# A sparse expert layer behind attention: the last batch's routing chain moved to earlier steps, pair numbers copied by another engine, the last combines paired

## The chip, the cores and the metric

The kernel runs on one core of a Trainium2 chip. The metric is the device time of one launch in microseconds. The median of three runs of the kernel before is 531.6 us (531.27 to 532.24).

## What is computed

The input x has 4 batches of 512 tokens with 256 features (2048 tokens). Three residual parts follow one another: half of a feed-forward layer, attention, and half of the same feed-forward layer again. Cut to what matters:

```
x = x + 0.5 * ffn(layernorm(x))
x = x + attention(layernorm(x))          # 3 heads, full 256 features each
x = x + 0.5 * ffn(layernorm(x))
ffn(x): scores = sigmoid(x @ gate_w)                     # 16 experts
        selected = top_2(scores + expert_bias)
        w = scores[selected] / sum(scores[selected])
        shared = silu(x @ sg) * (x @ su) @ sd            # every token
        routed = sum over the 2 selected e of w_e * (silu(x @ g_e) * (x @ u_e)) @ d_e
        return shared + routed
```

All products are done in three passes over a high and a low part of each float32 operand, so that they are near to full float32.

## The kernel before, in words

The work is written out by hand as one program for each of the five engines: TensorE (PE), VectorE (DVE), ScalarE (ACT), GpSimd (POOL) and SyncE (SP, which only issues DMAs). Each executes its list in order; semaphores tie them together. The change lies in the second feed-forward layer ("FFN 2"), behind the attention.

**Tiles.** The tokens are sorted by expert into tiles of 128 rows. With 2048 tokens and 2 experts each there are 47 tiles at most. FFN 2 handles them in two phases. Tiles 0 to 8 (`FULL_TILES` = 9) hold only tokens of batches 0 to 2 and can start before batch 3's experts are known. Tiles 9 to 46 hold the rest. In a loop step s (function `ffn` of each engine) PE transposes the rows of tile s, multiplies tile s - 1 by the expert's gate and up weights, transposes the product of tile s - 3 and multiplies tile s - 4 by the down weights. ACT copies the high parts and applies Silu; DVE makes the low parts and the products. ACT copies the result of a tile to `y_buf` (L1039), and POOL scatters it to `pair_dram` by pair number (`scatter_y`, L1935). `between(s)` at the end of a step runs side work.

**Rows.** The normalised rows of each token are written by indirect DMAs of POOL into slabs in DRAM, one slab for each expert (`slab_row`, L1906: 4 tiles of tokens, twice, as each token has two experts). Beside the 256 features a row holds its pair number, which POOL puts there first (`mark`, L1889 and L1890). SP loads one tile of rows at a time (`load_row`, L2114) into a ring of 4 buffers; the load of tile n waits until PE has transposed tile n - 4 and until `keep_id(n - 4)` (POOL, L1929) has copied that tile's pair numbers out of the buffer. Before the tiles of phase 2 are loaded, SP writes 17 blocks of zero rows behind the ends of the slabs (`clear_rest`, L2120 and L2126), once DVE has given their addresses (`zero_at`, L1360).

**Batch 3's routing chain** runs beside phase 1, as side work of the steps (function `late_front` on PE, ACT and DVE). In order: DVE normalises the 4 row tiles (L1224, step 1); PE transposes them (`late_turn`, steps 2 and 3), ACT and DVE split them (`front_hi` L919, `front_lo` L1253); PE multiplies by the router (`front_router`, step 4); ACT applies Sigmoid (`front_sigmoid`, L934, step 4) and at once a one-element Silu, to have Silu's table loaded again (L1063); PE transposes the scores (step 5); DVE picks the two experts (`choose`, steps 5 to 7); PE counts ranks (`rank_again`, step 8); DVE makes slab addresses (`slab_rows`, steps 8 and 9, ends at L1344) and the table of tiles (`tile_table(True)`, steps 10 and 11). PE turns the table over (`pack_table`, behind phase 1), DVE writes it (`write_table`, L1421).

**The shared expert.** The same engines handle the shared expert batch by batch: `shared_gu` (gate and up), ACT's `shared_silu`, DVE's `shared_mul` (L1261), `shared_hi` and `shared_lo` (L965, L1265), PE's `shared_y`, and DVE's `shared_sink` (L1278). PE does `shared_gu(1, 0)` in step 9 and `shared_gu(1, 1)` in step 10 of phase 1, and behind its last step 12 `shared_y(1, 0)`, `shared_gu(1, 2)`, `pack_table(True)`, `shared_y(1, 1)`, `shared_y(1, 2)`, and then phase 2. The inputs of batches 1 and 2 are reloaded from DRAM by SP (`reload_batch`, L2071); ACT copies their high part (`back_hi`, L925), and POOL makes the low part (`back_lo`, L1923), for which `shared_gu` of that batch waits.

**POOL's list in FFN 2** is: `keep_id` 0 to 3; `back_lo(1)`; `keep_id(4)`; `scatter_y(0)`; `keep_id(5)`; `scatter_y(1)`; `back_lo(2)`; `keep_id(6)`; `scatter_y(2)`; `keep_id` 7 and 8; `scatter_y(3)`; the 8 `slab_row`s; `scatter_y` 4 to 8; then one `keep_id` and one `scatter_y` for each tile of phase 2.

**The tail.** When 39 tiles are scattered, SP loads the pairs of the first 12 token tiles (`load_pair`, L2134, 256 KB each), when all 47 are, those of the last 4. DVE combines: two operations for each token tile (L1529), the second waiting for the first. SP stores each token tile to the output when it is combined (`tail2`, L2165).

## Time and profile before

| | us |
|---|---|
| median of 3 runs (531.27 to 532.24) | 531.6 |
| the profiled execution | 529.91 |
| its span, first to last instruction | 528.7 |
| PE busy in the span | 443.9 (84%) |
| DVE busy | 334.8 (63%) |
| POOL busy | 299.0 (57%) |
| ACT busy | 266.1 (50%) |

The mean granted clock of TensorE over the span is 0.956 of full speed. The profile is of one execution, taken by the hardware. Times are microseconds from the first instruction. PE is TensorE's matmuls, PEld its weight loads. SPq is the issue of a DMA on SP's queue. In the rows of a timeline, the first number is the start, the second the length (several alike are merged, their count is behind the x), and square brackets give the idle time ahead and what ended it.

### The profile page before, as it was taken

The page shows a single profiled execution, that of the slowest core. Times are in us where ns is not written, and L with a number is a line of the kernel's source. Part 1 is how long each engine was busy: PE and PEld are TensorE (multiplying, and loading weights), DVE is VectorE, ACT ScalarE, POOL GpSimd, SP SyncE. Part 2 cuts the span into 40 slices and gives each one's busy share as a digit, 9 for nine tenths or more (in the row PEclk, how much of TensorE's full clock was granted, in tenths as well). Part 3 has the DMA queues.
Part 4 walks back from the last instruction along what each step waited for, and adds up shares of the span by engine and source line. Part 5 has one row for each costly group of instructions (what it writes and reads, how often), then busy time and mean ns, then how long its engine had stood idle before and what let it go on. Part 6 is the DMA issues. An engine that isn't in the chain of part 4 may idle for free.

```text
span 528.7 us, 10108 instructions
## 1 busy us (share of the span) xinstructions
PE 443.9 (84%) x2951; PEld 392.7 (74%) x2951; DVE 334.8 (63%) x985; ACT 266.1 (50%) x706; POOL 299.0 (57%) x371
## 2 busy tenths in 40 slices
PE   1566699999877999999999999999977686999962
PEld 1335688999766889988898888988866674899951
DVE  6469575566457664377466855675756445776677
ACT  4855166676633545444444353544344631677740
POOL 5357675555064753475337548477572576578860
PEclk9967599999999999999999999999989999999996
DMA  8733445665632200011001111012015056455597
GB/s 297 275 104 120 140 128 186 207 197 139 168 90 68 60 2 0 11 52 40 21 1 51 41 32 57 28 61 105 22 64 164 32 188 211 125 166 166 186 311 247
DMA packets 44469, 60.34 MB, mean 114 GB/s; under 512 B 6080, under 2 KB 36800, under 8 KB 44416
## 3 DMA queue, kind: packets, MB, share of 16 engines
q1 hardware_dynamic: 36416, 38.68, 23.1%
q0 software_dynamic: 7584, 20.98, 12.8%
q8 instruction: 27, 0.44, 0.4%
q14 instruction: 26, 0.21, 0.1%
q10 hardware_dynamic: 416, 0.02, 0.1%
HBM read 34.75 MB, written 24.91 MB: 113 GB/s over the span
## 4 chain that ended last, share of the span: by engine, by line
PE 36%; DVE 11%; issue 10%; POOL 4%; DMA 3%; SPq 2%; ACT 2%; ACTq 0%; DVEq 0%; POOLq 0%
PE bank L394 32%; DVE x_sb L1529 3%; DMA stage<-slab_dram 2%; POOL pair_dram L1935 2%; PE bank L400 2%; POOL slot_i L1929 1%; SPq L2126 1%; DVE softmax_row L1762 1%; ACT v_sp L1172 1%; DVE x_sb L1635 1%; PE bank L424 1%; DVE v_sp L1776 1%; DVE stats L1205 1%; DVE raw L1224 1%; DVE route L1317 0%
## 5 line engine op out<-in xcount | busy, mean ns | idle before, releaser
L2008 POOL TENSOR_TENSOR e_sp<-raw,e_sp 128x512 fp32r<-128x512 f32 x48 | 62.3, 1299 | 68.9 <-ACT e_sp L1141 68.5
L394 PE MATMUL bank<-v_sp,e_sp 128*128 128x256 f32 x576 | 77.3, 284 | 1.9 <-DVE x_sb L1635 1.9
L394 PEld LDWEIGHTS bank<-v_sp,e_sp 128*128 128x128 f32 x576 | 74.6, 191 | 5.7 <-issue 2.7
L394 PE MATMUL bank<-g_sp,xT 128*128 128x512 f32 x288 | 75.9, 400 | 0.1
L1973 POOL DMA_INDIRECT raw<-xn_dram,gather_at x47 | 46.5, 989 | 31.4 <-PE bank L400 28.4
L394 PEld LDWEIGHTS bank<-g_sp,xT 128*128 128x128 f32 x288 | 52.5, 192 | 9.6 <-issue 0.2
L1164 ACT ACTIVATE raw<-bank,softmax_row 128x512 f32<-128x512 f32 x48 | 33.2, 692 | 52.5 <-DVE softmax_row L1762 52.1
L1935 POOL DMA_INDIRECT pair_dram<-raw,slot_i x47 | 47.5, 1010 | 16.5 <-issue 8.9
L1605 DVE TENSOR_TENSOR e_sp<-bank,e_sp 128x128 fp32r<-128x128 f32 x94 | 27.3, 291 | 41.7 <-ACT e_sp L1010 41.7
L394 PE MATMUL bank<-w_hi,e_sp 128*128 x188 | 51.6, 297 | 1.4 <-DVE e_sp L1605 1.1
L394 PE MATMUL bank<-b_sp,xT 128*128 128x256 f32 x288 | 44.5, 291 | 7.7 <-DVE v_sp L1776 7.5
L1762 DVE TENSOR_REDUCE softmax_row<-bank 128x1 f32<-128x512 f32 x48 | 32.9, 686 | 27.2 <-PE bank L394 26.7
L394 PE MATMUL bank<-w_hi,xt_late 128*128 x188 | 47.0, 312 | 1.5 <-DVE xt_late L1609 1.2
L394 PE MATMUL bank<-w_hi,xT 128*128 x188 | 46.0, 307 | 0.7 <-DVE xT L1609 0.6
L1776 DVE SCALAR_TENSOR_TENSOR v_sp<-bank,softmax_row,v_sp 128x256 fp32r<-128x256 f32 x48 | 23.2, 484 | 35.8 <-ACT v_sp L1172 35.8
L394 PEld LDWEIGHTS bank<-b_sp,xT 128*128 128x128 f32 x288 | 38.2, 192 | 10.2 <-DVE v_sp L1776 9.7
L1881 POOL DMA_INDIRECT stage<-y_dram,slot_i x32 | 32.3, 1008 | 21.8 <-DMA y_dram<-stage 14.1
L1027 ACT ACTIVATE raw<-bank 128x128 f32<-128x128 f32 x94 | 26.3, 280 | 28.6 <-PE bank L394 28.4
L394 PEld LDWEIGHTS bank<-w_hi,e_sp 128*128 128x128 f32 x188 | 35.9, 191 | 4.4 <-issue 3.7
L1614 DVE TENSOR_TENSOR raw<-raw,bank 128x128 f32<-128x128 f32 x94 | 27.0, 287 | 15.3 <-ACT raw L1027 11.2
L394 PE MATMUL bank<-xT,a_sp 128*128 128x512 f32 (+1 forms) x156 | 36.0, 378 | 0.8 <-DVE xT L1549 0.7
L394 PEld LDWEIGHTS bank<-w_hi,xt_late 128*128 128x128 f32 x188 | 33.8, 198 | 2.6 <-issue 2.3
(283 smaller groups left out, 1090.5 us busy)
## 6 DMA issues: line engine op xcount, KB each, us to landing
stage<-slab_dram SPq DMA_DIRECT2D x47, 136.0 KB
y_dram<-stage SPq DMA_DIRECT2D x47, 128.0 KB, 2.9
late_pair<-pair_dram SPq DMA_DIRECT2D x16, 256.0 KB, 5.0
slab_dram<-stage SPq DMA_DIRECT2D x17, 136.0 KB
stage<-in_w_pack SPq DMA_DIRECT2D x6, 384.0 KB, 5.1
raw<-in_w_pack SPq DMA_DIRECT2D x6, 384.0 KB, 3.2
x_sb<-in_x SPq DMA_DIRECT2D x4, 512.0 KB, 6.9
xn_dram<-xn_all SPq DMA_DIRECT2D x4, 512.0 KB, 4.7
```

Source lines behind the costliest of these rows:

```text
L394: m = pe.matmul(dst, lhs[k][l], rhs[k][r], start=(first and k == 0 and i == 0), stop=(last and k == n - 1 and i == 2), skip_group_check=True)
L1027: act.activation(h_buf[:, g % 2, :], bank[GU_BANKS[g % 2]][:, 0:F], ACT.Silu).then_inc(s_silu, 1)
L1164: act.activation(e32[:, i, :], bank[S_BANKS[i]][:], ACT.Exp, bias=row_max[:, i, :], accum_out=row_sum[:, i, :]).then_inc(s_exp, 1)
L1529: dve.scalar_tensor_tensor(out=x_sb[:, t, :], in0=pair_buf[:, n % PAIRS, :] if r == 0 else late_pair[:, t, k, :], scalar=weight[:, k, t:t ...
L1605: dve.tensor_tensor(ht_rows[:, v % 2, 1], bank[HT_BANK][:, 0:P], ht_rows[:, v % 2, 0].bitcast(F32), ALU.subtract).then_inc(s_hT_lo, 1)
L1614: dve.tensor_tensor(h_buf[:, g % 2, :], h_buf[:, g % 2, :], bank[GU_BANKS[g % 2]][:, F:GU], ALU.mult).then_inc(s_act, 1)
L1762: dve.tensor_reduce(row_max[:, i, :], bank[S_BANKS[i]][:], AX, ALU.max, negate=True).then_inc(s_max, 1)
L1776: dve.scalar_tensor_tensor(out=v_sp[:, i, 1, :], in0=bank[V_BANK][:, 0:H], scalar=row_inv[:, i, :], in1=v_sp[:, i, 0, :].bitcast(F32), op0 ...
L1881: pool.indirect_dma_start(pair_buf[:, n % PAIRS, :], None, y_dram, at).then_inc(s_pair[n % PAIRS], 16)
L1935: pool.indirect_dma_start(pair_dram, bass.IndirectOffsetOnAxis(ap=tile_id[:, j % (TOPK * NT):j % (TOPK * NT) + 1].bitcast(U32), axis=0), y ...
L1973: pool.indirect_dma_start(row_buf[0][:, n % ROWS, :], None, xn_dram, bass.IndirectOffsetOnAxis(ap=gather_at[:, n:n + 1], axis=0)).then_inc ...
L2008: pool.tensor_tensor(e_sp[:, i, 1, :], e32[:, i, :], e_sp[:, i, 0, :].bitcast(F32), ALU.subtract).then_inc(s_e_lo, 1)
```

## The change

It is made in five parts, all in FFN 2:

1. **Chain.** Batch 3's routing chain starts in step 0 in place of step 1. The transposes are in steps 1 and 2, the router in 3, the transposed scores, the whole of `choose` and `keep_score` in 4, the ranks and the whole of `slab_rows` in 5, the table in 6 and 7, `pack_table(True)` in 8 and `write_table(True)` in 9. ACT executes a one-element Sigmoid in step 2, the Sigmoid of the scores and the one-element Silu in step 3; `back_hi(1)` moves from step 5 to 6, `back_hi(2)` from 7 to 8.
2. **Pair numbers.** `keep_id` is executed by DVE at the start of each step, no longer by POOL.
3. **POOL's order.** The marks of the first half of the slab rows come at once (4 tiles), then `scatter_y` 0 and 1, the 8 `slab_row`s, `back_lo(1)`, `scatter_y` 2 to 4, `back_lo(2)`, and the other scatters. SP loads rows 0 to 5 ahead of `reload_batch(1)`, row 6 between it and `reload_batch(2)`.
4. **List operations.** `list_rest` (behind the attention's last steps) has its order changed and waits less often between its operations.
5. **Tail.** Combines are done for two token tiles alternately (`combine_two`), and ACT issues the output stores of token tiles 0 to 11; SP keeps those of 12 to 15.

The diff, cut to its core:

```diff
@@ PE
             def late_front(s):
-                if s == 2:
+                if s == 1:
                     late_turn(0)
+                elif s == 2:
+                    late_turn(1)
                 elif s == 3:
-                    late_turn(1)
+                    front_router(1, B - 1)
                 elif s == 4:
-                    front_router(1, B - 1)
+                    turn_scores(1, B - 1)
                 elif s == 5:
-                    turn_scores(1, B - 1)
+                    rank_again(B - 1)
                 elif s == 8:
-                    rank_again(B - 1)
+                    pack_table(True)
                 elif s == 9:
                     shared_gu(1, 0)
...
             shared_y(1, 0)
             shared_gu(1, 2)
-            pack_table(True)
             shared_y(1, 1)
@@ ACT
             def late_front(s):
-                if s == 2:
+                if s == 1:
                     front_hi(1, FRONT_PAIRS - 2)
-                elif s == 3:
+                elif s == 2:
                     front_hi(1, FRONT_PAIRS - 1)
-                elif s == 4:
-                    front_sigmoid(1, B - 1)
                     act.wait_ge(s_inv_sum, U)
                     act.wait_ge(s_warm, 2)
+                    act.activation(row_sum[:, 0], minus_half[:, 0:1], ACT.Sigmoid).then_inc(s_warm, 1)
+                elif s == 3:
+                    front_sigmoid(1, B - 1)
+                    act.wait_ge(s_warm, 3)
                     act.activation(row_sum[:, 0], minus_half[:, 0:1], ACT.Silu).then_inc(s_warm, 1)
-                elif s == 5:
+                elif s == 4:
+                    keep_score(1)
+                elif s == 6:
                     back_hi(1)
-                elif s == 6:
-                    keep_score(1)
-                elif s == 7:
+                elif s == 8:
                     back_hi(2)
...
+            for q in range(LATE_T):
+                act.wait_ge(s_comb, combined(q))
+                act.dma_start(out_rows[q], x_sb[:, q, :]).then_inc(s_out, 16)
@@ DVE
+            def combine_two(t0):
+                for k in range(TOPK):
+                    for t in (t0, t0 + 1):
...
+                        dve.scalar_tensor_tensor(out=x_sb[:, t, :], in0=late_pair[:, t, k, :],
+                                                 scalar=weight[:, k, t:t + 1], in1=x_sb[:, t, :], op0=ALU.mult,
+                                                 op1=ALU.add).then_inc(s_comb, 1)
...
+            def keep_id(j):
+                row = row_buf[1][:, j % ROWS, :]
+                dve.wait_ge(s_row_late[j % ROWS], row_value(j))
+                dve.tensor_scalar(tile_id[:, j % (TOPK * NT):j % (TOPK * NT) + 1], row[:, H + 1:H + 2], float(j),
+                                  row[:, H:H + 1], ALU.mult, ALU.add).then_inc(s_id, 1)
...
                 for s in range(lo, hi + LAG):
                     g, v = s - 1, s - H_LAG
+                    if r == 1 and s < hi:
+                        keep_id(s)
...
             def late_front():
-                yield
                 dve.wait_ge(s_rstd[2], B)
...
-                yield from choose(1, LATE_T, NT)
-                yield from slab_rows(B - 1)
+                run(choose(1, LATE_T, NT))
+                yield
+                run(slab_rows(B - 1))
+                yield
                 yield from tile_table(True)
+                yield
+                write_table(True)
...
             ffn(1, between2, 0, FULL_TILES)
             shared_lo(1, 1)
-            write_table(True)
             shared_sink(1, 0)
@@ POOL
-            for j in range(ROWS):
-                keep_id(j)
-            back_lo(1)
-            keep_id(4)
-            scatter_y(0)
...
+            pool.wait_ge(s_g, 2 * B * HEADS)
+            for t in range(LATE_T, NT):
+                mark(late_rows[:, t - LATE_T, :], t, True)
+            for j in range(2):
+                scatter_y(j)
             for k in range(TOPK):
                 for t in range(LATE_T, NT):
                     slab_row(t, k)
-            for j in range(4, FULL_TILES):
+            back_lo(1)
+            for j in range(2, 5):
                 scatter_y(j)
-            for s in range(FULL_TILES, NI + LAG):
-                if s < NI:
-                    keep_id(s)
-                if s - LAG >= FULL_TILES:
-                    scatter_y(s - LAG)
+            back_lo(2)
+            for j in range(5, NI):
+                scatter_y(j)
@@ SP
-            for n in range(ROWS):
+            for n in range(ROWS + 2):
                 load_row(n, rows)
             reload_batch(1)
+            load_row(ROWS + 2, rows)
             reload_batch(2)
```

## Rows read from the trace of the kernel before

**Rows 1.** Timeline of PE, FFN 2's phase 1 and start of phase 2.

```profile
408.57 1.56 PE L394 MATMUL bank<-xT,gate_sp 128*16 128x512 f32 x6
...
419.48 0.44 PE L400 MATMUL bank<-ident,stage 128*128 128x128 f32 x2 [2.80 <-DMA stage<-slab_dram]
...
427.00 0.63 PE L394 MATMUL bank<-x_front,w_hi 128*128 128x512 f32 x2
...
433.08 0.39 PE L394 MATMUL bank<-w_hi,a_sp 128*128 128x256 f32 x1 [1.68 <-DVE a_sp L1265]
...
441.43 0.38 PE L394 MATMUL bank<-w_hi,a_sp 128*128 128x256 f32 x1 [2.04 <-DVE a_sp L1265]
...
444.69 0.44 PE L400 MATMUL bank<-ident,stage 128*128 128x128 f32 x2 [1.56 <-DMA stage<-slab_dram]
...
453.10 0.38 PE L400 MATMUL bank<-ident,stage 128*128 128x128 f32 x2
```

**Rows 2.** Timeline of SP's DMA issues: the zero blocks and phase 2's rows.

```profile
428.80 10.59 SPq L2126 DMA_DIRECT2D slab_dram<-stage  x16
442.26 10.32 SPq L2114 DMA_DIRECT2D stage<-slab_dram  x9
```

**Rows 3.** Waits of all engines from 453 to 503 (total us, times, longest).

```profile
PE bank L400 <- DMA stage<-slab_dram: 1.0, 2, 0.6
```

**Rows 4.** Timeline of POOL in phase 1.

```profile
401.59 1.05 POOL L1849 TENSOR_TENSOR rstd<-variance,columns 128x4 f32<-128x4 f32 x1 [4.43 <-DVE variance L1221]
...
414.29 2.38 POOL L1923 TENSOR_TENSOR x_front<-x_front 128x1024 fp32r<-128x1024 f32 x1 [10.64 <-ACT x_front L925]
...
426.78 1.00 POOL L1906 DMA_INDIRECT slab_dram<-xn_all,lane  x1 [0.28 <-POOL xn_all L1890]
...
432.81 0.98 POOL L1906 DMA_INDIRECT slab_dram<-xn_all,lane  x1 [0.28 <-POOL xn_all L1890]
```

**Rows 5.** Timeline of DVE in phase 1.

```profile
403.61 1.38 DVE L1224 TENSOR_SCALAR xn_all<-x_sb,moments,rstd 128x256 f32<-128x256 f32 x4
...
413.39 0.22 DVE L1299 TENSOR_TENSOR route<-bank,bias_sb 128x64 f32<-128x64 f32 x1
...
417.16 0.23 DVE L1322 TENSOR_TENSOR choice<-route 128x64 f16<-128x64 f32 x1
...
424.18 0.17 DVE L1344 CAST lane<-tile_sb 128x8 int32<-128x8 f32 x1
...
437.80 0.19 DVE L1421 TENSOR_SCALAR table<-bank 1x40 int32<-1x40 f32 x1 [2.82 <-PE bank L574]
```

**Rows 6.** Timeline of ACT in phase 1: table loads around the Sigmoid.

```profile
409.00 1.28 ACT L934 ACT_TABLE_LOAD   x1
...
410.89 1.28 ACT L1063 ACT_TABLE_LOAD   x1
```

**Rows 7.** Timeline of POOL: its last scatter.

```profile
511.08 0.98 POOL L1935 DMA_INDIRECT pair_dram<-raw,slot_i  x1 [0.30 <-issue]
```

**Rows 8.** Windows: us, busy us (instructions) of PE, PEld, DVE, ACT, POOL; granted clock, DMA share, GB/s.

```profile
448.00:450.00 2.00, 2.00 (x12) 2.00 (x12) 0.71 (x2) 0.69 (x3) 0.27 (x1) 0.52 0.34 84
...
512.00:514.00 2.00, 0.00 (x0) 0.00 (x0) 1.93 (x5) 0.59 (x1) 0.06 (x1) 1.00 1.06 382
...
516.00:518.00 2.00, 1.31 (x6) 1.32 (x7) 1.93 (x6) 0.00 (x0) 0.00 (x0) 0.59 0.03 10
```

**Rows 9.** Timeline of DVE in an undisturbed step of phase 2.

```profile
505.32 0.29 DVE L1605 TENSOR_TENSOR e_sp<-bank,e_sp 128x128 fp32r<-128x128 f32 x1 [0.33 <-ACT e_sp L1010]
```

**Rows 10.** Timeline of ACT: the copy of the last tile's result.

```profile
508.87 0.37 ACT L1039 COPY raw<-bank 128x256 f32<-128x256 f32 x1 [0.58 <-PE bank L394]
```

**Rows 11.** Timeline of SP's DMA issues in the tail: pair loads, stores.

```profile
502.72 16.18 SPq L2134 DMA_DIRECT2D late_pair<-pair_dram  x16
518.94 8.21 SPq L2165 DMA_DIRECT2D out<-x_sb  x16
```

**Rows 12.** Timeline of DVE: the last eight combines.

```profile
521.41 3.75 DVE L1529 SCALAR_TENSOR_TENSOR x_sb<-late_pair,weight,x_sb 128x256 f32<-128x256 f32 x8
```

135 lines of the change are left out of this document (67 added, 68 removed).

## The prediction

> **What bounds the kernel now.** The page's busy shares are averages, so I read the stages: first PE's timeline, then that of the engine it waits for. PE's timeline of FFN 2 shows three stretches. Phase 1 has waits: 2.80 us for row tile 8, 1.68 and 2.04 us for the shared expert's low parts; phase 2 begins at 444.69, where PE waited 1.56 us for rows [rows 1]. Those rows were issued at 442.26, behind 16 blocks of zeros that SP issued in 10.59 us from 428.80 [rows 2]. So phase 2's start is set by the routing chain through its addresses; but PE itself came free only at 443.13 (the 1.7 us of the last shared product from 441.43), so at most 1.6 us are there without shortening PE's own list. From 453 to 503 PE waits for rows twice, 1.0 us in all [rows 3]: there it is PE that sets the pace (1.40 us a tile where nothing disturbs), though POOL is close to it. The tail, from 503, is transfers and combines.
>
> **When the addresses are ready.** The four normalising operations start when POOL's rstd is there, 402.64 (401.59 + 1.05), and no longer in step 1 [rows 4]; before they started at 403.61 [rows 5]. That is 0.9 us gained, and three `keep_id`s of some 0.17 us each (a one-column DVE operation, estimated from L1344's 0.17 us [rows 5]) take little of it back, so the router starts at 407.8, not 408.57 [rows 1], and ends at 409.3 (1.5 long). ACT decides what follows. Before, two table loads of 1.28 us each stood there, at 409.00 and 410.89, and ACT went on at 412.4 (410.89 + 1.28 and an element's 0.2) [rows 6]. The change puts a one-element Sigmoid into step 2, but step 3 begins with the Silu of tile 2, and the Sigmoid of the scores comes only after it. So there are four loads in place of two: Sigmoid from 406.9 to 408.3 with its one element; two copies, 0.5; Silu load 1.28 and Silu 0.28, to 410.4; Sigmoid load 1.28 and 0.59 for the scores, 412.3; Silu load with its element 1.5, 413.8. The two added loads cost 2.6 us, and they lie on the chain, as only the end of the router (409.3) could have covered them.
>
> The trace has each load at 1.28 us, with nothing but the Sigmoid itself between the first and the second (1.89 apart, of which 0.61 isn't load) [rows 6]. By the Trainium skill, page "ScalarE: Activation LUTs", section "What ACT_TABLE_LOAD costs", a switch of sets costs 2.66 us with its drain; by that the two added ones would be 5.3 us, and the time would come out 2.7 us higher. The row decides here: I take 1.28.
>
> From the Silu on, one step's copies lead to `choose` in 1.0 us (412.4 to 413.39 [rows 5, 6]), `choose` is 1.95 us of operations in three pieces of 0.62 to 0.67, which lay over three steps to 417.39 [rows 5] and are now in one; DVE's three operations of the next step take 0.9, under which the ranks go; `slab_rows` is 1.25. 413.8 + 1.0 + 1.95 + 0.9 + 1.25 = 418.9, against 424.35 before (L1344's end [rows 5]). Moving the chain by up to four steps thus gives 5.4 us.
>
> **What POOL makes of it.** The two scatters ahead are through at 417.8. The slab rows start at 418.95 and not at 426.78 [rows 4]. The first four follow at 1.27 us (0.98 and 0.30 of issue, as two indirect DMAs with nothing between [rows 7]), the others at 1.46 (0.98, 0.28 of idle time and a copy of 0.2 [rows 4]): 10.9 us, to 429.9. The zero blocks' addresses come at 420; they take 11.6 and land 2.9 later, 434.6; the table is written at 425. So phase 2's rows can be loaded 7 us earlier than now. But `back_lo(1)` is now behind the eight slab rows. It takes 2.38 us and was done at 416.67 [rows 4]; now it ends at 432.35. `shared_gu(1, 1)` waits for it on PE, and behind that stand, in PE's list, the last three steps of phase 1, all three `shared_y`, and phase 2. Before it began at 427.00 [rows 1]. This is the wait that takes the place of the old one. `back_lo(2)`, three scatters later, ends at 438.8 and is in time for `shared_gu(1, 2)`.
>
> **From there to phase 2.** From `shared_gu(1, 1)` to phase 2 PE needed 17.7 us (444.69 - 427.00 [rows 1]). Of it 1.6 was the wait for rows and goes. The 2.82 us that DVE waited at 437.80 for the turned table, with `shared_mul(1, 2)` behind it [rows 5], go too: the multiply can start with the end of its product, and the 2.04 us wait at 441.43 [rows 1] shrinks to 0.3, 1.7 less. 14.4 remain: 432.35 + 14.4 = 446.8. PE is idle for 3.9 us ahead of this (`shared_gu(1, 0)` ends near 428.4). After waits of 2.80 and 1.56 us [rows 1] its granted clock went to the lower level (1.2 GHz) for parts of some 4 us: 0.52 in 448 to 450 [rows 8]. With 3 us at half speed I add 1.5 (bounds 0 and 2). Phase 2 starts at 448.3, 3.6 us later than before.
>
> **Phase 2.** Its first five tiles took 8.4 us (444.69 to 453.10 [rows 1]), with waits for rows and the low clock. With rows in the buffers and a warm clock the first ones need 6.0: 2.4 less. Later the 1.0 us of waits for rows [rows 3] and 0.3 around them go, since DVE gives the ring's buffers free at the start of a step; DVE has 0.33 us idle in an undisturbed step of 1.40 [rows 9] and `keep_id` fits in (if it doesn't, each of 38 steps pays up to 0.1). DVE's weights still hold PE up as before. POOL at 1.27 us a tile no longer trails: its last scatter starts at 511.08, 1.8 us behind the last copy (509.24) [rows 7, 10].
>
> **Tail.** For the same reason the pair loads (502.72 [rows 11]) begin 1.5 us nearer to PE's last tile. SP's 16 stores go out back to back for 8.21 us, the last 1.1 us after the last combine ended at 525.16 [rows 11, 12]; with ACT issuing 12 of them, this queue is gone, 1.5 less. Pairing the combines takes 0.1 from each second one, up to 1.6, but from tile 12 on they wait for their loads, so little of it counts. Against this, the ACT stores run while the first 12 loads and the last scatters still fill the DMA engines (1.06 at 382 GB/s [rows 8]); 1.05 MB of them is 3.0 us at 350 GB/s. They push back the last 4 loads by as much as is not moved into the hole at 516 to 518 (0.03, 10 GB/s [rows 8]). I take 1.0 back. Tail: -2.0 (bounds +1 and -4). By the Trainium skill, page "DMA: Bandwidth & Descriptors", section "Queues, rings and completion order", each DMA engine takes the queue rows with work in turn; by that ACT's stores would not stand behind SP's loads but slow them, which is the collision that I price.
>
> `list_rest` ends behind the attention, where PE's matmuls cover it; should it count, it is some 0.5 us either way. The marks of the first four tiles are done while POOL waits.
>
> **Sum.** +3.6 (phase 2's start) - 2.4 (its first tiles) - 1.3 (waits for rows) - 2.0 (tail) = -2.1 us. The profiled execution of before, 529.91 with a span of 528.7, would be 527.8 with a span of 526.6. The median lies 1.7 above the profiled one; I keep that: 531.6 - 2.1 = 529.5. A measurement of this kernel can tell some 0.2% (1.06 us) from no change.
>
> **Rivals.** (a) The added table loads don't come, or POOL's order doesn't hold PE: the addresses are 2.6 us earlier, PE isn't cold, so phase 2 starts near 444.2, and the gain is 6.2: 525.4. For it speaks that all of this hangs on one order of instructions; against it, that Silu and Sigmoid each forced a load in the rows. 0.15. (b) The forecast's mechanism with a full tail gain, or with all terms a little better or worse, 527 to 530.5: 0.45. (c) The gains and losses cancel, 530.5 to 532.7: the tail gives nothing, as it is bound by 6.3 MB of transfers that are the same. 0.2. (d) Slower: `shared_gu(1, 1)` waiting for `back_lo(1)`. Each microsecond by which the addresses come later moves phase 2 by as much. The addresses come later where PE's low clock already strikes in steps 4 and 5 (two waits of 1.6 us each there), a product of 0.8 us then takes 1.4, and twice that in a row is 1.2; with the whole 2 us of slow clock behind the POOL wait phase 2 starts at 450.0, +5.3. With - 2.4 - 1.3 and a tail of only -0.3 the sum is +1.3: 532.9, and up to 535 if the tail loses its +1. With that tail it decides from phase 2's start at 449.8 on. 0.2.
>
> The range that leaves out 2 in 10 is 525.0 to 533.5. Faster by over 0.2%: (a) and all but 0.02 of (b), 0.58; same: (c) and that rest, 0.22; slower: (d), 0.20. The likeliest case alone: 527.5 to 530.5.
>
> **What would show it.** In the profile of after: four ACT table loads between 401 and 415 behind the first Silu's (if only two, the address term is wrong); L1344 ending near 419; the first L1906 near 419 and back-to-back; L1923 near 430; PE idle for about 4 us ahead of `shared_gu(1, 1)`, put down to POOL, with a clock below 1 after it; no DMA wait at phase 2's first transpose, which lies near 448; L1929's work now on DVE at some 0.2 us and PE's pace still 1.40; L1935 at the heels of L1039; the last stores on ACT's and SP's queues within 2.5 us of the last combine. If phase 2 starts before 445, rival (a) was right; if DVE's steps exceed 1.40 us, my cover for `keep_id` was wrong.

## The result, and the profile after

The changed kernel takes 527.92 us (median of 10 runs, 525.62 to 532.46), the kernel before beside it 531.75 (10 runs). The ratio is 0.9945, with an interval of 0.9922 to 0.9968: 2.9 us faster (1.7 to 4.1). The two medians alone lie 3.8 us apart; the ratio is worked out from all executions of both kernels and has an interval, so it stands for every version below. The prediction was 529.5 in 525.0 to 533.5, 2.1 us faster. The profiled execution took 527.82 us with a span of 526.6; the prediction had 527.8 and 526.6. Of all executions below, one of e9 (1078.31 us) and one of e12 (1463.51 us) took two to three times as long as the rest; they are in no ratio and no median.

The page of after, part 1 (busy us, share of the span, instructions) and the heading of part 4 (the chain that ended last):

```profile
PE 444.0 (84%) x2951; PEld 393.2 (75%) x2951; DVE 337.5 (64%) x1031; ACT 267.8 (51%) x709; POOL 283.7 (54%) x324
...
PE 42%; DVE 10%; issue 4%; POOL 4%; ACT 3%; DMA 3%; SPq 0%; ACTq 0%; DVEq 0%; POOLq 0%
```

POOL lost 15 us of busy time, DVE gained 3, and PE stayed at 444. These sums don't tell where 2 us of the span went; the stages do. First the routing chain. Timeline of ACT in phase 1, table loads and what they load for:

```profile
406.48 1.28 ACT L1064 ACT_TABLE_LOAD   x1
407.77 0.20 ACT L1064 ACTIVATE softmax_row<-columns 128x1 f32<-128x1 f32 x1
...
408.42 1.28 ACT L1030 ACT_TABLE_LOAD   x1
409.72 0.28 ACT L1030 ACTIVATE raw<-bank 128x128 f32<-128x128 f32 x1
410.01 1.28 ACT L937 ACT_TABLE_LOAD   x1
411.31 0.59 ACT L937 ACTIVATE xn<-bank 16x512 f32<-16x512 f32 x1
411.91 1.28 ACT L1068 ACT_TABLE_LOAD   x1
413.20 0.20 ACT L1068 ACTIVATE softmax_row<-columns 128x1 f32<-128x1 f32 x1
```

Four loads stand where two stood [rows 6], each at 1.28 us, and the operation behind a load starts 0.01 to 0.02 us after it. The one-element Sigmoid of L1064 brings a table that the Silu of L1030 throws out again before the Sigmoid of L937 needs it. Nevertheless the addresses are ready 5.9 us earlier than before (424.35). Timeline of DVE, the last operation of the addresses:

```profile
418.30 0.17 DVE L1353 CAST lane<-tile_sb 128x8 int32<-128x8 f32 x1
```

What POOL makes of it is in its timeline: first and last slab row, both `back_lo` (L1963), a scatter (L1969) before and after:

```profile
417.40 0.96 POOL L1969 DMA_INDIRECT pair_dram<-raw,slot_i  x1 [1.30 <-ACT raw L1042]
418.75 0.96 POOL L1946 DMA_INDIRECT slab_dram<-xn_all,lane  x1 [0.38 <-DVE lane L1353]
...
428.36 0.98 POOL L1946 DMA_INDIRECT slab_dram<-xn_all,lane  x1 [0.28 <-POOL xn_all L1930]
429.37 2.35 POOL L1963 TENSOR_TENSOR x_front<-x_front 128x1024 fp32r<-128x1024 f32 x1
431.88 1.00 POOL L1969 DMA_INDIRECT pair_dram<-raw,slot_i  x1 [0.17 <-issue]
...
435.43 2.38 POOL L1963 TENSOR_TENSOR g_sp<-g_sp 128x1024 fp32r<-128x1024 f32 x1
```

And PE waits for it. PE's timeline at `shared_gu(1, 1)` and at the start of phase 2 (447.50), tile 14 (453.84):

```profile
427.53 0.28 PE L397 MATMUL bank<-w_hi,e_sp 128*128 x1
431.77 1.22 PE L397 MATMUL bank<-x_front,w_hi 128*128 128x512 f32 x2 [3.96 <-POOL x_front L1963]
...
447.50 0.60 PE L403 MATMUL bank<-ident,stage 128*128 128x128 f32 x4
...
453.84 0.38 PE L403 MATMUL bank<-ident,stage 128*128 128x128 f32 x2
```

Two matmuls of the same kind took 0.63 us before [rows 1] and take 1.22 here. The windows (columns as in [rows 8]) show that the granted clock fell to its lower level (1.2 GHz, 0.50) behind the wait of 3.96 us:

```profile
430.00:432.00 2.00, 0.23 (x1) 0.23 (x2) 0.00 (x0) 0.00 (x0) 1.83 (x2) 0.82 0.82 287
432.00:434.00 2.00, 2.00 (x5) 1.59 (x6) 0.00 (x0) 0.00 (x0) 1.70 (x2) 0.50 0.20 70
434.00:436.00 2.00, 2.00 (x9) 1.52 (x8) 0.00 (x0) 0.60 (x1) 1.67 (x3) 0.83 0.80 236
436.00:438.00 2.00, 1.23 (x8) 0.83 (x6) 0.29 (x1) 0.96 (x4) 1.83 (x2) 1.00 0.59 173
```

So phase 2 starts 2.8 us later than before (444.69 [rows 1]). SP had its rows ready long before; the zero blocks went out 8 us earlier. SP's timeline:

```profile
420.76 9.89 SPq L2151 DMA_DIRECT2D slab_dram<-stage  x16
433.25 0.94 SPq L2139 DMA_DIRECT2D stage<-slab_dram  x2
```

From phase 2's start on, the changed kernel gains; the table below has the stages. The tail: SP's loads and stores, then ACT's stores, then POOL's last scatter, ACT's last copy and DVE's last combines, from the four timelines:

```profile
501.68 16.67 SPq L2159 DMA_DIRECT2D late_pair<-pair_dram  x16
521.47 3.70 SPq L2187 DMA_DIRECT2D out<-x_sb  x4
...
511.79 7.39 ACTq L1196 DMA_DIRECT2D out<-x_sb  x12
...
510.20 1.28 POOL L1969 DMA_INDIRECT pair_dram<-raw,slot_i  x1 [0.30 <-issue]
...
508.23 0.37 ACT L1042 COPY raw<-bank 128x256 f32<-128x256 f32 x1 [0.58 <-PE bank L397]
...
522.84 1.89 DVE L1553 SCALAR_TENSOR_TENSOR x_sb<-late_pair,weight,x_sb 128x256 f32<-128x256 f32 x4 [1.00 <-DMA late_pair<-pair_dram]
```

### The profile page after: what moved, and what is told of

The parts are those of the page before. It is cut to its first block, busy times and chain, and to the rows that moved or that the text cites. A ratio compares the mean times of both kernels' runs of the same rounds, so it can differ in the third digit from the quotient of the medians.

```text
span 526.6 us, 10094 instructions
## 1 busy us (share of the span) xinstructions
PE 444.0 (84%) x2951; PEld 393.2 (75%) x2951; DVE 337.5 (64%) x1031; ACT 267.8 (51%) x709; POOL 283.7 (54%) x324
## 3 DMA queue, kind: packets, MB, share of 16 engines
HBM read 34.75 MB, written 24.91 MB: 113 GB/s over the span
## 4 chain that ended last, share of the span: by engine, by line
PE 42%; DVE 10%; issue 4%; POOL 4%; ACT 3%; DMA 3%; SPq 0%; ACTq 0%; DVEq 0%; POOLq 0%
PE bank L397 37%; PE bank L403 2%; POOL slab_dram L1946 2%; DVE softmax_row L1803 1%; DMA pair_dram<-raw,slot_i 1%; DMA late_pair<-pair_dram 1%; DVE x_sb L1666 1%; PE bank L427 1%; ACT v_sp L1177 1%; DVE x_sb L1539 1%; PE bank L674 1%; DMA slab_dram<-stage,lane 1%; DVE stats L1214 1%; DVE v_sp L1817 1%; DVE raw L1233 1%
## 5 line engine op out<-in xcount | busy, mean ns | idle before, releaser
L397 PE MATMUL bank<-v_sp,e_sp 128*128 128x256 f32 x576 | 78.6, 287 | 2.5 <-DVE x_sb L1666 1.9
L397 PEld LDWEIGHTS bank<-v_sp,e_sp 128*128 128x128 f32 x576 | 75.7, 194 | 6.3 <-issue 2.7
L397 PE MATMUL bank<-g_sp,xT 128*128 128x512 f32 x288 | 74.8, 395 | 0.1
L1969 POOL DMA_INDIRECT pair_dram<-raw,slot_i x47 | 45.8, 974 | 46.5 <-ACT raw L1042 32.4
L1030 ACT ACTIVATE raw<-bank 128x128 f32<-128x128 f32 x94 | 26.3, 279 | 28.3 <-PE bank L397 28.3
```

What stands on the lines that cost most here:

```text
L397: m = pe.matmul(dst, lhs[k][l], rhs[k][r], start=(first and k == 0 and i == 0), stop=(last and k == n - 1 and i == 2), skip_group_check=True)
L1030: act.activation(h_buf[:, g % 2, :], bank[GU_BANKS[g % 2]][:, 0:F], ACT.Silu).then_inc(s_silu, 1)
L1969: pool.indirect_dma_start(pair_dram, bass.IndirectOffsetOnAxis(ap=tile_id[:, j % (TOPK * NT):j % (TOPK * NT) + 1].bitcast(U32), axis=0), y ...
```

## The experiments

Each was timed in five rounds against the kernel before. As executions differ by up to 3 us in what lies ahead of FFN 2, the table counts from FFN 2's first transpose (T0) in each profile. The stages: the end of the addresses, `shared_gu(1, 1)`, the transposes of tiles 9 (start of phase 2), 14 and 46 (the last), and the end of the span.

| kernel | ratio to before | addresses | shared_gu(1, 1) | tile 9 | 9 to 14 | 14 to 46 | 46 to end | T0 to end |
|---|---|---|---|---|---|---|---|---|
| before | 1 | 24.43 | 27.08 | 44.77 | 8.41 | 50.16 | 25.44 | 128.78 |
| after | 0.9945 | 18.78 | 32.08 | 47.81 | 6.34 | 48.79 | 23.97 | 126.91 |
| e1_two_loads | 0.992 | 17.81 | 31.08 | 48.58 | 6.34 | 48.71 | 23.60 | 127.23 |
| e2_back_lo_first | 0.9908 | 21.06 | 30.79 | 46.79 | 6.34 | 48.69 | 23.31 | 125.13 |
| e3_tail_only | 0.997 | 24.62 | 26.95 | 45.13 | 8.50 | 50.32 | 24.12 | 128.07 |
| e4_ids_only | 0.9931 | 24.91 | 25.98 | 44.32 | 8.22 | 48.75 | 25.43 | 126.72 |
| e5_pool_early | 0.9884 | 18.52 | 27.80 | 44.25 | 6.38 | 48.54 | 23.95 | 123.12 |
| e6_early_two_loads | 0.9825 | 16.53 | 25.58 | 41.90 | 6.34 | 48.68 | 23.95 | 120.87 |
| e7_single_combines | 0.997 | 18.96 | 32.22 | 49.57 | 6.34 | 48.65 | 24.15 | 128.71 |
| e8_sp_stores | 1.0014 | 18.70 | 32.00 | 50.52 | 6.34 | 48.82 | 24.80 | 130.48 |
| e12_changed_again | 0.9944 | 20.25 | 33.56 | 52.04 | 6.38 | 48.87 | 23.50 | 130.79 |
| e11_no_cast | 0.9874 | 21.0 | 31.16 | 45.42 | 6.34 | 48.71 | 24.42 | 124.89 |
| e9_scatter2_between | 0.9786 | 16.82 | 26.10 | 40.35 | 6.34 | 48.66 | 23.33 | 118.68 |
| e13_ids_and_tail | 0.9888 | 23.35 | 24.42 | 43.58 | 8.73 | 48.77 | 22.83 | 123.91 |

Behind the ratio, which is of all executions, a row shows a single one. How far a single one can be trusted is shown by the rows "after" and e12, which are the same code: they differ by 1.5 us at `shared_gu(1, 1)`, by 4.2 at tile 9, by 0.5 in the last stage and by 3.9 in the sum; only the two stages from tile 9 to 46 repeat within 0.1. A smaller difference in another column says little unless a timeline shows the wait that made it. The row "before" is also one of the faster executions of its kernel (529.91 us, where the medians beside the versions are 531.15 to 532.66), so the columns show less gain than the ratios: its granted clock is 1.00 from 430 to 448, where e3, e4 and e13, whose chain stands in the same steps, have 0.50 to 0.53 for a part of it.

### Without the added table loads

```diff
@@ ACT late_front, step 2
-                    act.activation(row_sum[:, 0], minus_half[:, 0:1], ACT.Sigmoid).then_inc(s_warm, 1)
```

> The changed kernel without the one-element Sigmoid of step 2, so two table loads instead of four. My theory (the added loads lie on the chain: addresses -> eight slab rows -> back_lo(1) -> shared_gu(1, 1) -> phase 2): ACT goes on near 411.5 and not 413.3, the last address operation (L1353 of the changed kernel) comes 1.8 to 1.9 us earlier, shared_gu(1, 1) near 429.9, phase 2's first transpose near 445.6 in place of 447.50, and the whole is 1.9 us shorter than the changed kernel (ratio to before near 0.991). Rival 1 (loads hidden behind the router): addresses unchanged, time unchanged. Rival 2 (the tail is set by transfers): phase 2 starts 1.9 us earlier, but under 0.5 us reaches the end.

Measured: 527.38 us, ratio 0.992 (0.9897 to 0.9943): 1.3 us less than the changed kernel where 1.9 was expected, with intervals that overlap. Two loads went. In this profile the addresses came only 1.0 us earlier, as the router itself was late (granted clock 0.50 from 404 to 408 and 0.55 to 410, behind a wait of 1.50 us; 1.00 in all of this in the changed kernel's profile), and phase 2 started at 449.95, not at 445.6: the profile doesn't show the gain. The second try, e6 against e5 below, has it undisturbed: the addresses 2.0 us earlier, phase 2 2.35 us earlier, and ratios whose intervals don't touch. The loads are on the chain, at 2.0 to 2.35 of their 2.56 us.

### back_lo(1) ahead of the slab rows

```diff
@@ ACT late_front
-                elif s == 6:
+                elif s == 5:
                     back_hi(1)
@@ POOL
             for j in range(2):
                 scatter_y(j)
+            back_lo(1)
             for k in range(TOPK):
                 for t in range(LATE_T, NT):
                     slab_row(t, k)
-            back_lo(1)
```

> The changed kernel with back_hi(1) in step 5 and back_lo(1) ahead of the eight slab rows on POOL, nothing else. My theory (POOL's place of back_lo(1) holds PE for 4 us): PE's idle time of 3.96 us ahead of shared_gu(1, 1) is gone, it starts near 428, its clock stays high. But POOL's scatter 2 and back_lo(2) now end 2.4 us later relative to the slab rows: the copy of tile 8's result waits for scatter 2 to land (near 435), and shared_gu(1, 2) for back_lo(2) (near 438), so 2.5 us of the 5 are given back: phase 2 starts near 445, the whole is 2.5 us shorter than the changed kernel (ratio to before near 0.990). Rival (the slab rows and not back_lo set phase 2): they land 2.4 us later, phase 2 starts 2.4 us later than 447.5 and the time is 2.4 us longer.

Measured: 526.86 us, ratio 0.9908 (0.9874 to 0.9941): 2.0 us less than the changed kernel by the ratios, near the 2.5 expected, with intervals that overlap. But `shared_gu(1, 1)` hardly moved (30.79 in place of 32.08; at 430.86 where 428 was expected), and the addresses came 2.3 us later. Timeline of DVE and of POOL:

```profile
418.29 0.29 DVE L1352 TENSOR_REDUCE tile_sb<-reach 128x8 f32<-128x128 f32 x1
418.61 2.52 DVE L1353 CAST lane<-tile_sb 128x8 int32<-128x8 f32 x1
421.05 0.20 DVE L1624 TENSOR_SCALAR slot_i<-stage 128x1 int32<-128x1 f32 x1
...
418.74 2.35 POOL L1963 TENSOR_TENSOR x_front<-x_front 128x1024 fp32r<-128x1024 f32 x1
421.42 0.98 POOL L1946 DMA_INDIRECT slab_dram<-xn_all,lane  x1 [0.32 <-DVE lane L1353]
```

A cast of 8 columns took 2.52 us where it takes 0.17; it ended at 421.13, 0.04 us behind the end of POOL's `back_lo`, which ran beside it. PE, waiting for DVE's `e_sp`, stood still too (2.49 us). So moving the operation exchanged one wait for another; a place for it where DVE has nothing of that kind to do was needed.

### The tail alone

```diff
@@ on the kernel before
-            for t in range(TB):
-                combine(1, t)
+            for t in range(0, TB, 2):
+                combine_two(t)
...
+            for q in range(LATE_T):
+                act.wait_ge(s_comb, combined(q))
+                act.dma_start(out_rows[q], x_sb[:, q, :]).then_inc(s_out, 16)
```

> The kernel before with the tail alone changed: combines of two token tiles alternately, ACT issuing the stores of tiles 0 to 11. Up to the pair loads nothing changes (they start near 502.7). My theory: the queue of stores on SP goes (1.5 us), 0.5 to 1 is taken back by stores that run beside the loads: 0.5 to 1.0 us shorter, ratio 0.998 to 0.999. Rival (transfers bound): no difference, 1.000. Rival (collision wins): 0.5 to 1.5 us longer.

Measured: 530.24 us, ratio 0.997 (0.9941 to 0.9999): -1.6 us, more than the 0.5 to 1.0 expected, with an interval that all but reaches no change. From tile 46 to the end it is 1.3 us less.

### The pair numbers alone

```diff
@@ on the kernel before, DVE
+                    if r == 1 and s < hi:
+                        keep_id(s)
@@ POOL
-            for j in range(ROWS):
-                keep_id(j)
             back_lo(1)
-            keep_id(4)
             scatter_y(0)
-            keep_id(5)
             scatter_y(1)
...
```

> The kernel before with keep_id on DVE alone; the routing chain, POOL's order of the rest and the tail stay. My theory: row tile 8 no longer waits (2.80 us), the addresses come 2.8 us earlier, so zero blocks and slab rows too, and PE is free 2.8 us earlier; phase 2 starts near 442 (before 444.69; changed 447.50), its waits for rows (1.3) go, and POOL's last scatter follows the last copy at once (1.5): 4 to 5.5 us shorter than before, ratio near 0.991, that is more than the whole change gives. Rival (the gain of the change comes from the moved chain): under 2 us, ratio above 0.996, as phase 2 still waits for the zero blocks.

Measured: 527.9 us, ratio 0.9931 (0.9906 to 0.9955): -3.7 us, a little under the 4 to 5.5 expected, and no less than the whole change gives. The waits of PE from 450 to 503 in this kernel (total us, times, longest) hold no row wait any more [rows 3]; this is all of them:

```profile
PE bank L672 <- DVE e_sp L1613: 1.9, 2, 1.2
```

Tiles 14 to 46 take 1.4 us less, `shared_gu(1, 1)` is 1.1 us earlier (the wait of 2.80 us for row tile 8 is gone [rows 1]), and the tail is the same as before to 0.01 us. Two steps of the expectation failed. The tail gave nothing, where 1.5 us were expected. And the addresses came 0.5 us later than before, not 2.8 earlier, so that phase 2 started 0.45 us earlier, not 2.8. One reason is in the timelines of DVE and POOL:

```profile
424.80 1.26 DVE L1341 TENSOR_TENSOR reach<-route,lane_no 128x128 f32<-128x128 f32 x1
...
423.50 2.40 POOL L1931 TENSOR_TENSOR g_sp<-g_sp 128x1024 fp32r<-128x1024 f32 x1
```

DVE's `reach`, on the way to the addresses, took 1.26 us in place of 0.29 and ended 0.16 us behind POOL's `back_lo(2)`: the same kind of hold as in e2, begun in the middle of POOL's operation. e13 has it too (1.26 us, from 421.35).

### Both of them, without the moved chain

Run last of all. The two edits above together; the chain, the list operations and POOL's order are those of before.

> The kernel before with keep_id on VectorE and the paired combines and ACT stores, the routing chain of batch 3 and the spread list operations left as they were. It tells what the moved chain is worth in the changed kernel: this kernel and the changed one differ by the chain, the list operations and POOL's order alone. Theory A (the two parts add up, and the moved chain costs time because back_lo(1) now stands behind the slab rows): the gains of e4 (0.9931) and e3 (0.997) add to a ratio of 0.990 (0.988 to 0.992), 526.9 us beside 532.0, and the changed kernel's 0.9944 is some 2.3 us behind it; the profile shows phase 2's tile 9 at 44.3 us from FFN 2's first transpose, tile 14 to 46 in 48.7, and 24.1 from there to the end, 1.3 less than e4's. Theory B (the two gains share a cause, the late end of POOL's scatters, so that they don't add): 0.993 to 0.995, and the moved chain is worth nothing either way.

Measured: 525.93 us, ratio 0.9888 (0.9851 to 0.9925); theory A. The gains add (3.7 + 1.6 = 5.3; measured 6.0). In the profile the last stage is 22.83 us where 24.1 was expected; why isn't known. The changed kernel differs from this one by the moved chain, the list operations and POOL's order, and it is slower: 0.9945 (0.9922 to 0.9968) and 0.9944 (0.9915 to 0.9973) in two comparisons, against 0.9851 to 0.9925 here. The intervals overlap at the edge; by the middles it is 3.0 us. In the stages of the profiles: phase 2 starts 4.2 us later, its first five tiles win back 2.4. The list operations were never timed alone, so their share of the 3.0 isn't known.

### back_lo(1) in POOL's idle time

```diff
@@ ACT late_front
-                elif s == 6:
-                    back_hi(1)
@@ POOL
+            pool.wait_ge(s_back[1], 16)
+            pool.tensor_copy(front_x[1][1][:, 0], front_x[1][1][:, 1].bitcast(F32)).then_inc(s_back_hi1, 1)
+            back_lo(1)
             for j in range(2):
                 scatter_y(j)
...
-            back_lo(1)
```

> The changed kernel with batch 1's high and low part both made on POOL in its idle time ahead of scatter 0 (ACT's back_hi(1) goes), so that back_lo(1) no longer stands behind the slab rows and doesn't run beside DVE's cast of the addresses. My theory (back_lo(1)'s place costs PE 4 us and the low clock after it): the slab rows start where they did (19.1 us after FFN 2's first transpose), shared_gu(1, 1) starts without a wait 28.2 us after it (changed 32.1), phase 2 42.8 us after it (changed 47.8), and the whole is 4 to 5 us shorter than the changed kernel: ratio to before 0.985 to 0.987. Rival (another chain stands close behind: scatter 2's landing, back_lo(2), the zero blocks): under 2 us shorter, ratio above 0.990, with a PE wait elsewhere.

Measured: 524.97 us, ratio 0.9884 (0.9858 to 0.9909). POOL's timeline and PE's:

```profile
407.48 1.04 POOL L2052 CAST x_front<-x_front 128x1024 fp32r<-128x1024 f32 x1 [4.48 <-DMA x_front<-xT_dram]
408.60 2.37 POOL L1962 TENSOR_TENSOR x_front<-x_front 128x1024 fp32r<-128x1024 f32 x1
...
427.26 0.28 PE L398 MATMUL bank<-w_hi,e_sp 128*128 x1
427.38 0.63 PE L398 MATMUL bank<-x_front,w_hi 128*128 128x512 f32 x2
```

No wait of PE and no low clock at `shared_gu(1, 1)`: two matmuls take 0.63 us again. The gain is less than the 4 to 5 us expected, and phase 2 starts at 44.25, not at 42.8: behind a later wait of 2.32 us for `a_sp` the granted clock was 0.53 and 0.62 from 434 to 438. Phase 2 starts 3.56 us earlier than in the changed kernel, where PE's wait was 3.96 us, and the ratio is 0.0061 lower (3.2 us). This is the direct measurement of the wait that took the place of the old one.

### The same, with two table loads

e5 and e1 together.

> As e5, and the one-element Sigmoid of step 2 left out as in e1. My theory: PE's steps come 1 to 1.9 us earlier, and as nothing else holds shared_gu(1, 1), phase 2 starts 41 to 42 us after the first transpose: 1 to 1.9 us shorter than e5, ratio 0.982 to 0.985. Rival (the table loads only mattered through the addresses, which no longer bind): no difference to e5.

Measured: 521.99 us, ratio 0.9825 (0.9793 to 0.9857), as expected; against e5 it is 3.1 us by the ratios and 2.35 at phase 2. With the wait and the two loads away, the version with the moved chain is 3.3 us faster than e13, which leaves the chain where it was (0.9888; the intervals overlap by 0.0006). So the earlier place of the chain is a gain where nothing behind it pays for it.

### The combines one after another

```diff
@@ the changed kernel, DVE combine_two
-                for k in range(TOPK):
-                    for t in (t0, t0 + 1):
+                for t in (t0, t0 + 1):
+                    for k in range(TOPK):
```

> The changed kernel with the combines of one token tile after the other, as before; ACT still stores. My theory (from tile 12 on the combines wait for their loads): each pair costs 0.92 us in place of 0.80, but the last combine ends within 0.3 us of the changed kernel's place behind the last load: 0 to 0.4 us longer, ratio 0.9945 to 0.9955. Rival (DVE bound tail): 1.6 us longer, ratio 0.9975.

Measured: 530.16 us, ratio 0.997 (0.9944 to 0.9997), against 0.9945 with pairs. Eight combines in a row take 3.75 us here and 3.25 in pairs; the last four, which wait for their loads, take 1.92 here and 1.89 in pairs. The tail (46 to end) is 0.2 us longer than in the changed kernel's first profile and 0.65 longer than in its second (e12). The other stages hold no combines; phase 2 starts 1.8 us later here than in the first profile and 2.5 earlier than in the second. The ratio of 0.997 is nearer to the rival's, but its interval overlaps the changed kernel's. What the pairing is worth at the end isn't measured to better than some tenths; the 0.5 us of each eight is mostly hidden behind the loads.

### All stores by SP

```diff
@@ the changed kernel, ACT
-            for q in range(LATE_T):
-                act.wait_ge(s_comb, combined(q))
-                act.dma_start(out_rows[q], x_sb[:, q, :]).then_inc(s_out, 16)
@@ SP
-                for q in range(LATE_T, NT):
+                for q in range(NT):
```

> The changed kernel with all output stores issued by SP, as before; the combines stay paired. My theory: the stores queue behind the last pair load again, 16 at 0.49 us each, and the end comes 1.4 us later from the issue of the 13th pair load (11.7 us in place of 10.3), though that issue is 0.3 us nearer: 1.0 to 1.4 us longer than the changed kernel, ratio 0.9965 to 0.997. Rival (transfers bound): same time as the changed kernel.

Measured: 532.5 us, ratio 1.0014 (0.998 to 1.0048). SP's timeline in the tail:

```profile
521.16 7.94 SPq L2183 DMA_DIRECT2D out<-x_sb  x16
```

The queue is back (7.94 us for 16 stores, 0.50 each), and the tail is 0.8 us longer than in the changed kernel (1.3 longer than in its second profile); from the 13th pair load on it is 11.28 in place of 10.29. But the ratio moved by 0.0069, 3.7 us, and the profile's phase 2 began 2.7 us later than the changed kernel's, though the stores are issued only behind phase 2. This sent me to the next run.

### The changed kernel again

> The changed kernel once more, beside the next two. Ratio to before 0.992 to 0.997, as in the first comparison. Its stretch from FFN 2's first transpose to phase 2's first should be 47.8 us where the low clock behind POOL's wait lasts as long as in the first profile, up to 50.5 where it lasts longer.

Measured: 529.40 us (11 runs), ratio 0.9944 (0.9915 to 0.9973), as before. But its profile isn't: the same code has phase 2 at 52.04 and not at 47.81, beyond the 50.5 that was expected at most. Of these 4.2 us, 1.5 lie ahead of `shared_gu(1, 1)`: the granted clock was 0.50 from 402 to 406 and 0.58 to 408, where the first profile has 1.00, and the router and the addresses came later by as much. The rest lies behind the POOL wait (4.08 us here). The windows there:

```profile
434.00:436.00 2.00, 2.00 (x6) 1.59 (x5) 0.00 (x0) 0.46 (x1) 1.70 (x2) 0.50 0.60 153
436.00:438.00 2.00, 2.00 (x7) 1.41 (x6) 0.00 (x0) 0.14 (x1) 1.98 (x2) 0.50 0.84 279
...
442.00:444.00 2.00, 2.00 (x10) 2.00 (x10) 1.36 (x3) 0.51 (x1) 1.25 (x2) 0.50 0.20 70
```

The clock stayed at the lower level to 438 and fell again at 442. From `shared_gu(1, 1)` to phase 2 it is 15.7 us in the first profile of this code, 18.5 in this one. The same stretch took 17.50 in e1, 17.35 in e7 and 18.52 in e8, which wait for POOL there too (3.0 to 4.1 us): the first profile is the shortest of the five. With the clock at 1.00 all through it is 14.25 (e9) and 14.26 (e11). What the clock costs behind the wait is thus 1.5 to 4.3 us, and single profiles can't weigh edits of a microsecond across it. That e8's ratio is off by more than its tail isn't explained by this alone, for it is of 12 executions and its interval doesn't touch either one of the changed kernel. The mean granted clock of these 12 is 0.948, that of the changed kernel's 21 is 0.953, and within those 21 an execution with 0.01 less is some 2.3 us longer (a straight line through the 21); by that estimate the clock has about 1.1 of the 3.7 us and the tail 0.8 to 1.3. Why the clock was lower, and the rest, stays open.

### The cast away

```diff
@@ e2_back_lo_first, DVE slab_rows, batch 3
-                dve.tensor_reduce(tile_sb[:, t0:t1], reach[:], AX, ALU.add)
-                dve.tensor_copy(addr_i[:, :, t0:t1], tile_sb[:, t0:t1])
+                dve.tensor_reduce(addr_i[:, :, t0:t1], reach[:], AX, ALU.add)
```

> As e2 (back_lo(1) ahead of the slab rows), but batch 3's addresses are written as whole numbers by the reduction itself, so the copy that changed their type, which took 2.52 us in e2 and 0.17 us elsewhere, is gone. Theory A (that copy was held by POOL's two-input operation running beside it): the last address operation ends 18.5 us after FFN 2's first transpose (e2: 21.06), the slab rows start where they did in e2 (POOL is busy with back_lo(1) until then), shared_gu(1, 1) starts 28.3 us after it (e2: 30.79), and the whole is 2 us shorter than e2: ratio near 0.987. Theory B (any DVE operation on SBUF alone is held by POOL's): the next such operation, keep_id(6), takes 2.3 us in its place, nothing is gained, ratio 0.991.

Measured: 526.12 us, ratio 0.9874 (0.9846 to 0.9902). DVE's timeline and POOL's:

```profile
419.03 0.17 DVE L1347 TENSOR_TENSOR slab_to<-slab_to,bank 128x16 f32<-128x16 f32 x1
419.24 2.57 DVE L1350 TENSOR_TENSOR reach<-route,lane_no 128x128 f32<-128x128 f32 x1
...
419.27 2.38 POOL L1967 TENSOR_TENSOR x_front<-x_front 128x1024 fp32r<-128x1024 f32 x1
```

Now it is the operation ahead of the cast that is held, 2.57 us in place of 0.29. `shared_gu(1, 1)` is where it was (31.16 and 30.79). So the theory that the cast alone is special fell. The other, that what comes next is held, holds of `reach` (two inputs in SBUF), and not, as it had it, of `keep_id`: one of those ran its 0.21 us in the middle of POOL's operation in e5. In e5's timeline of DVE, beside POOL's operation of 2.37 us from 408.60:

```profile
409.85 0.21 DVE L1623 TENSOR_SCALAR slot_i<-stage 128x1 int32<-128x1 f32 x1
```

The ratio is the 0.987 that theory A had, but not by its mechanism: the addresses came at 21.0, not at 18.5. It lies below e2's (0.9908), with intervals that overlap. In the profiles phase 2 starts 1.4 us earlier than in e2, and that goes with the clock: it was granted at 0.58 and 0.56 of full speed from 438 to 442 in e2 and at 1.00 from 428 on in e11. Whether the edit or the execution made this difference isn't settled.

### Scatter 2 between the slab rows: the best version

```diff
@@ e6_early_two_loads, POOL
             for k in range(TOPK):
                 for t in range(LATE_T, NT):
                     slab_row(t, k)
-            for j in range(2, 5):
-                scatter_y(j)
+                if k == 0:
+                    scatter_y(2)
             back_lo(2)
-            for j in range(5, NI):
+            for j in range(3, NI):
                 scatter_y(j)
```

> As e6, with scatter 2 between the two halves of the slab rows and back_lo(2) right behind them. In e6 ACT's copy of tile 8's result waits for scatter 2 to land, and PE's wait ahead of the first shared_y is 2.19 us, where it is 1.68 elsewhere. My theory: that wait goes back to 1.68 and the low clock behind it is shorter: 0.5 to 1.5 us less than e6, ratio 0.9795 to 0.9815; the slab rows end 1.3 us later at no cost, since phase 2's rows have 8 us to spare. Rival (rows become late): phase 2's first transpose waits for a DMA.

Measured: 520.51 us (5 runs), ratio 0.9786 (0.9754 to 0.9819): 11 us faster than the kernel before, 8 faster than the changed one, and a little better than expected. Against e6 it is 2.1 us by the ratios, with intervals that overlap. ACT's copy of a tile's result waited 1.17 us in e6 for a scatter to free its buffer (timeline of ACT, e6, then e9):

```profile
430.36 0.37 ACT L1043 COPY raw<-bank 128x256 f32<-128x256 f32 x1 [1.17 <-DMA pair_dram<-raw,slot_i]
```

```profile
430.45 0.37 ACT L1043 COPY raw<-bank 128x256 f32<-128x256 f32 x1 [0.65 <-PE bank L398]
```

PE's wait for `a_sp` behind it shrank from 2.19 to 1.68 us, and PE, whose longest wait from 418 to 450 is this one, has its full clock; e6 had 0.67 and 0.50 from 432 to 436. From `shared_gu(1, 1)` to phase 2 it is 14.25 us against 16.32 in e6: 0.5 of the difference is the shorter wait, and the rest goes with the clock. Windows of e9:

```profile
420.00:430.00 10.00, 9.33 (x55) 7.65 (x54) 3.46 (x14) 4.84 (x13) 7.49 (x12) 1.00 0.90 311
430.00:440.00 10.00, 7.55 (x49) 6.65 (x49) 5.90 (x10) 2.63 (x5) 7.82 (x7) 1.00 0.43 139
```

## Why the prediction was right

The mechanism was right: the chain's addresses came earlier, four table loads stood in it, `back_lo(1)` behind the slab rows held PE for 4 us, and the first tiles, the rows and the tail won more than that cost. The sum of -2.1 us lies in the measured interval (1.7 to 4.1 us faster). That the span of 526.6 came out to the tenth is luck: ten executions spread from 525.62 to 532.46 us, and the second profile of the same code has a span of 529.8. The profile's stages add up to -1.87 from T0 and -0.23 ahead of it (+3.04 - 2.07 - 1.37 - 1.47 - 0.23 = -2.10); those of the second profile, e12, to +2.0 from T0, with +7.3 at phase 2. The code is the same; the granted clock isn't. The median was forecast 1.7 us above the profiled execution, as before; it is 0.1 above it, so 529.5 is 1.6 too high. Term by term:

- **Addresses.** 418.9 forecast, 418.47 in the profile. The four loads came in the order that the prediction read from the code, at the row's 1.28 us. The Trainium skill, page "ScalarE: Activation LUTs", section "What ACT_TABLE_LOAD costs", has 2.66 us for a switch, 1.28 of it the load and the rest a drain. The trace agrees on the load (1.28 us) and shows no drain: the load at 410.01 starts 0.01 us behind the operation ahead of it, and the next operation 0.02 us behind the load. e6 against e5 prices two of them at 2.0 us at the addresses and 2.35 at phase 2.
- **back_lo(1).** End at 432.35 forecast, 431.72 in the profile; PE idle 3.9 forecast, 3.96 in the profile. e5, which takes the wait away and leaves PE's list as it is, has phase 2 3.56 us earlier and a ratio 3.2 us lower. This is shown.
- **Start of phase 2.** +3.6 forecast, +3.0 from T0 in the profile. The 14.4 us from `shared_gu(1, 1)` to phase 2 at full clock are right: 14.25 in e9 and 14.26 in e11. The clock term of 1.5 us fits this execution (15.7 us) by luck: the other four profiles with this wait have 17.35 to 18.52, a clock term of 3.1 to 4.3. The bound of 2 us above it was too narrow.
- **First tiles.** -2.4 forecast, -2.07 in the profile. Rows were there, clock 1.00. Every kernel with the moved chain has 6.34 to 6.38; before, e3, e4 and e13 have 8.2 to 8.7.
- **Row waits.** -1.3 forecast, -1.37 in the profile, and e4 has the same (-1.41) by the pair numbers alone. `keep_id` took 0.207 us each and fitted in DVE's idle time of 0.33 us a step [rows 9]: an undisturbed tile still takes 1.40 us. One cost was not seen: DVE's weights now hold PE 1.24 and 0.63 us (0.96 and 0.49 before). DVE's groups from 455 to 500 (busy us, mean ns):

```profile
L1624 DVE TENSOR_SCALAR slot_i<-stage 128x1 int32<-128x1 f32 x30 | 6.2, 207 | 0.0
```

- **Tail.** -2.0 forecast, -1.47 in the profile, -1.94 in e12's. The failed part is "POOL no longer trailing", 1.5 us: the last scatter starts 1.60 us behind the end of the last copy (510.20 - 508.60), before 1.84 (511.08 - 509.24 [rows 7, 10]), and from tile 46 to the 13th pair load it is 13.68 us against 13.74. e4, with the pair numbers alone, has the same tail as before. I read a lag as a backlog without looking at whether it grew over the steps. The store queue was worth 1.4 us (11.70 to 10.29 from the 13th load to the end; 1.0 by e8's 11.28), near the 1.5 forecast; the row read for it was read wrong, though, as the last store is issued at 526.71, 1.55 us behind the last combine [rows 12] and not 1.1. The collision, priced on 1.05 MB where 12 stores of 128 KB are 1.57, cost 0.2 to 0.4 us, not 1.0: the 13th pair load waits for the last scatter, and it is issued 6.11 us behind that scatter's start (6.29 in e12), against 5.92 before and 5.96 in e8, where ACT stores nothing. ACT's stores began only at 511.8, behind ACT's own last `shared_hi`. The pairing was little, as forecast. By the Trainium skill, page "DMA: Bandwidth & Descriptors", section "Queues, rings and completion order", each DMA engine takes the queue rows with work in turn; the 0.2 to 0.4 us agree with sharing, and with the stores not standing behind the loads.
- **What the prediction didn't see** is how the parts stand to each other. It had the moved chain at about -2.4 + 3.6 = +1.2 beside the two others at -3.3. Measured, the two others alone are -6.0 (e13), and the chain with the list operations and POOL's order costs 3.0 of it. So the two groups were mis-sized by 2.7 and by 1.8 us in opposite directions, and it is luck that the sum stayed near. A change of 0.55% hid one of 1.1%, which a version with POOL's order put right turned into 2.1%.

Of the rivals, (a) needed that POOL doesn't hold PE and that two loads don't come: that is e6, forecast 6.2 us faster, measured 9.3. (d), slower, needed phase 2 at 449.8: e12's profile has it at 451.05 (399.01 + 52.04), with a span of 529.8 against 528.7. So by phase 2's start single executions of this kernel fall on (d)'s side; the median doesn't.

## What to carry to other kernels

When a chain is moved earlier in a kernel with in-order queues, look at what it is now ahead of: eight indirect DMAs that were late on POOL became eight that stand in front of an operation that PE needs, and a gain of 5.9 us at the addresses became a loss of 2.8 at phase 2 (447.50 against 444.69). Where a change has several parts, time each alone and all but one: here the parts were worth -3.7, -1.6 and, by difference, +3.0, and only that showed where to go on (-11 us). Profile the same code twice before a stage is compared. Put a one-element activation that is to warm a table directly ahead of its use, with no activation of another table between.

## What was not expected of the hardware

- **VectorE is held by GpSimd for whole operations.** Beside a GpSimd tensor_tensor of 2.35 to 2.38 us, a DVE cast of 128x8 took 2.52 us (elsewhere 0.17), and a DVE tensor_tensor with both inputs in SBUF 2.57 (elsewhere 0.29). Where the tensor_tensor began in the middle of GpSimd's operation (e4 and e13), it took 1.26 us and ended 0.15 to 0.16 behind it. A one-column tensor_scalar from float32 to int32 took its 0.21 us in the middle of such a GpSimd operation (e5, at 409.85), and a tensor_tensor with one of its inputs in PSUM its usual 0.17 (`slab_to` in the kernel before, at 421.70). The Trainium skill, page "SBUF — State Buffer", section "SBUF: two separate sides", tells of a pair of ports that the two engines share under an exclusive lock, taken by a DVE operation in a two-port mode or with two inputs in SBUF. The rows of `reach` agree with it, and so does the one with an input in PSUM; in which mode the cast and the tensor_scalar ran no row shows. The section gives the pair to whichever starts first; in e2 and e11 DVE's row starts 0.13 and 0.03 us before GpSimd's, and yet DVE was the one held. It matters when POOL's operation is put beside a chain of small DVE operations: one of 0.17 us can cost 2.5.
- **What the clock does behind a wait differs between executions.** After the same wait of 4 us in the same code the granted clock was 0.50 from 432 to 434 and 0.83 from 434 to 436 in one profile, and 0.50 from 432 to 438 and again from 442 to 444 in another. The stretch to phase 2 took 15.73 and 18.48 us, and 14.25 where the clock was 1.00 all through (e9).
- **A GpSimd cast of 128x1024 to fp32r takes 1.04 us** (e5, at 407.48), its tensor_tensor of the same size 2.37.
